# A two-layer transformer block with routed experts: choices of former tiles summed on TensorE, and the last tables loaded and added in quarters

## The chip, the cores and the metric

One core of a Trainium2 chip. The metric is the device time of one execution in microseconds (us). The engines are TensorE (PE, with its weight loads as PEld), VectorE (DVE), ScalarE (ACT), GpSimd (POOL) and SyncE (SP, which issues most DMAs).

## What is computed

1024 tokens (4 sequences of 256) of 256 features go through two layers. Each layer norms its input and adds an attention and a feed-forward part to it:

```
x = L0_attn_h                                   # (4, 256, 256), f32
xn = layernorm(x)
x = x + attention0(xn) + experts0(xn)           # 32 experts, 6 a token, 2 shared ones
xn = layernorm(x)
x = x + attention1(xn) + experts1(xn)           # 8 experts, 2 a token
return x

# experts0:  p = softmax(flat @ router_w + router_b); top 6, gates divided by their sum
#            out = mean of shared experts + sum of gate * (relu(flat @ w1 + b1) @ w2 + b2)
# experts1:  top 2 of x @ gate_kernel, softmax over the two;
#            h = silu(x @ wi_0) * (x @ wi_1) * weight;  out = h @ wo
# attention1: per token, 16 heads of q meet 8 heads of k through sine and cosine
#             features of rotated, normed vectors; the result @ Wo.T + bo
```

## The kernel before

Tokens stand in NT = 8 tiles of 128, two tiles a sequence. The kernel does not run every expert on every token. It sorts the chosen (token, expert) pairs into tiles of 128 slots of one expert each: NT0 = 79 tiles in layer 0, NT1 = 23 in layer 1. GpSimd gathers the tokens of a tile from a table in HBM (`gather_tile` L930, `gather_tile1` L1170), TensorE and ScalarE compute the expert, and GpSimd scatters the result with an addition into one of two tables of sums (`add_tile` L938, `add_tile1` L1177), tile n into table n % 2. A scatter waits for the former one on the same table.

**The routing** (`route_dve`, `rank_pe`, `route_dve_slots`, both layers; E is 32 or 8). VectorE finds each token's top experts (L264, L267), lays them out as zeros and ones (L271), and reduces them to CUM, for each tile E columns that are 1 where the token chose the expert (L274). MASKB is CUM in bf16 (L277). CUM is then summed over the tiles, each tile added to the sum of those before it, seven links (L281), and CUMB is that sum in bf16, shifted by a tile so that its first block is zero (L279, L283). `st` counts an instruction on a semaphore, and `st.link` also waits for it, so each link waits for the one before. The last conversion sets `chosen`. TensorE (`rank_pe`) then forms, in one bank, for each tile the number of earlier tokens of the tile that chose the expert (BEFOREB, a triangular matrix of ones, times the tile's block of MASKB, L377) plus those of all former tiles (ONESB, all ones, times the tile's block of CUMB, L379), and after them the total of each expert (L381), 17 matmuls in all. The last sets `rank_ok`. VectorE (`route_dve_slots`) normalises the gates (L295 to L297), waits for `rank_ok`, turns the totals into first slots of each expert (L301 to L310), and adds both up to the slot of each pair (L311 to L321). In layer 1, the rotation of queries and keys (`rope_qk`, L1074, six instructions for the first half of the tokens, each pair waiting for a square by ScalarE, L1069) stands between `route_dve` and `route_dve_slots`, and TensorE's `queries_keys` (L1063) of the second half waits for it through `qk_rp`. The slots then give the map from slot to token (L1134 to L1164), whose last instruction sets `map_ok` and lets GpSimd gather.

In layer 0, TensorE's program is: shared expert first product (L1876), its second product for two tiles `shared_down(0)` (L1884, L1885), `rank_pe`, `shared_down(1)`, the query compression (L1899), and then the map loop. In layer 1 it is: `queries_keys(0, 2)`, `rank_pe`, `queries_keys(1, 0)`.

**The end** (the last part of `layer1_dve` and the SP program). When an attention output of layer 1 has been multiplied for a sequence b (`project1`, L1349, sets `ao_ps`), VectorE adds it to the residual X (`take_project1`, L1356, 128 x 512). SP waits until all scatters of a table are in (`added[r]`) and loads the table of sums into SUMS1 in one DMA of 1 MB (L1629); it does so for both tables. VectorE does three projection adds, then adds the first table (L1490, 128 x 2048), then the second in four pieces of two tiles (L1494), each setting `f_ok`, and then the fourth projection add. SP stores each sequence when `f_ok` says so, the last when `ao_rd` says that the fourth projection is added, too (L1635).

Of the kernel before, what the change touches and what calls it, by code (L numbers as in the profile page):

```python
# [8 lines left out]
BF16 = mybir.dt.bfloat16  # L9
# [116 lines left out]
def build(nc, a, out):  # L126
# [5 lines left out]
    with ctx:  # L132
# [39 lines left out]
        MASKB = sb("chosen_bf16", NT * E0, BF16)  # L172
# [83 lines left out]
        def route_dve(dve, st, E, K, layer):  # L256
# [16 lines left out]
            st.wait()  # L273
            st.link(nc.vector.tensor_reduce(v3(CUM[:, 0:NT * E], NT),  # L274
                                            ONEH[:, 0:NT * K * E].rearrange("p (t k e) -> p t e k", t=NT, k=K),
                                            AX, ALU.add))
            st(nc.vector.tensor_copy(MASKB[:, 0:NT * E], CUM[:, 0:NT * E]))  # L277

            st.link(nc.vector.memset(CUMB[:, 0:E], 0.0))  # L279
            for t in range(1, NT):  # L280
                st.link(nc.vector.tensor_tensor(CUM[:, t * E:(t + 1) * E], CUM[:, (t - 1) * E:t * E],  # L281
                                                CUM[:, t * E:(t + 1) * E], ALU.add))
            nc.vector.tensor_copy(CUMB[:, E:(NT + 1) * E], CUM[:, 0:NT * E]).then_inc(chosen, 1)  # L283
# [89 lines left out]
        def rank_pe(pe, E, bank, layer):  # L373

            pe.wait_ge(chosen, layer + 1)
            for t in range(NT):
                nc.tensor.matmul(bank[:, t * E:(t + 1) * E], BEFOREB[:, :], MASKB[:, t * E:(t + 1) * E],  # L377
                                 start=True, stop=False)
                nc.tensor.matmul(bank[:, t * E:(t + 1) * E], ONESB[:, :], CUMB[:, t * E:(t + 1) * E],  # L379
                                 start=False, stop=True)  # L380
            nc.tensor.matmul(bank[:, NT * E:(NT + 1) * E], ONESB[:, :], CUMB[:, NT * E:(NT + 1) * E],  # L381
                             start=True, stop=True).then_inc(rank_ok, 1)
# [666 lines left out]
        sum1_ld, f_ok, f_st = [sem(f"sums1_loaded{i}") for i in range(2)], sem("f_combined"), sem("f_stored")  # L1049
# [303 lines left out]
        def take_project1(dve, b):  # L1353
            dve.wait_ge(ao_ps, b + 1)
            x = X[:, b * TPB * HID:(b + 1) * TPB * HID]
            return nc.vector.tensor_tensor(x, ps[PROJB[b % 2]][:, :], x, ALU.add).then_inc(ao_rd, 1)  # L1356
# [72 lines left out]
        def layer1_dve(dve, st):  # L1429
# [53 lines left out]
            for b in range(B - 1):  # L1483
                take_project1(dve, b)
            dve.wait_ge(ao_rd, B - 1)
            for i in range(2):
                r = (NT0 + NT1 + i) % 2
                dve.wait_ge(sum1_ld[r], 16)
                if i == 0:
                    st.link(nc.vector.tensor_tensor(X[:, :], X[:, :], SUMS1[r], ALU.add))  # L1490
                else:
                    for b in range(B):
                        x, y = (z[:, b * TPB * HID:(b + 1) * TPB * HID] for z in (X[:, :], SUMS1[r]))
                        ins = nc.vector.tensor_tensor(x, x, y, ALU.add)  # L1494
                        ins.then_inc(f_ok, 1)
            dve.wait_ge(f_ok, B)
            take_project1(dve, B - 1)


        with nc.Block() as block:  # L1500
            @block.sync
            def _(sp):
# [123 lines left out]
                for i in range(2):  # L1626
                    r = (NT0 + NT1 + i) % 2
                    sp.wait_ge(added[r], in_ring(NT0 + NT1, 2, r))
                    sp.dma_start(v3(SUMS1[r], NT), sums1[r][0:T, :].rearrange("(t p) d -> p t d", p=P)).then_inc(sum1_ld[r], 16)  # L1629
                rows = out.rearrange("b (j p) d -> b p j d", p=P)  # L1630
                for b in range(B):
                    sp.wait_ge(f_ok, b + 1)
                    if b == B - 1:
                        sp.wait_ge(ao_rd, B)
                    sp.dma_start(rows[b], x3[:, b * TPB:(b + 1) * TPB, :]).then_inc(f_st, 16)  # L1635
# [381 lines left out]
```

## Time and profile before

| | |
|---|---|
| median of three runs | 561.8 us (559.34 to 562.46) |
| the profiled execution | 560.66 us, its span 558.9 us |
| TensorE busy | 517.5 us, 93% |
| VectorE busy | 358.5 us, 64% |
| ScalarE busy | 314.5 us, 56% |
| GpSimd busy | 297.3 us, 53% |
| DMA | 90.41 MB, mean 162 GB/s |
| granted TensorE clock, mean | 0.985 |

The profile is of one execution. Busy time says how full an engine is, not what an instruction of it costs the kernel. For that one reads the chain that ended last (followed back from the last instruction, at each step to what released it) and, around a line, the timeline with the idle time that its engine had before it and who ended it. Matmuls overlap: each lasts some 0.18 us longer than the distance to the next. An f32 matmul shows as two instructions.

### The profile page before, as it was taken

To read this page: it belongs to the slowest core of one execution; us is meant where nothing else is said; L and a number is where in the kernel's file an instruction comes from. 1 tells how busy PE (TensorE), PEld (TensorE's weight loads), DVE (VectorE), ACT (ScalarE), POOL (GpSimd) and SP (SyncE) were. 2 spreads that over 40 slices of the span, in tenths; PEclk is the share of its full clock that TensorE was granted. 3 is DMA by queue.
4 is the path that set the end of the run, shared out by engine and by line. 5 is a ranking of instruction groups with operands and counts; after the bars stand their busy time and mean duration, and the time that the engine had idled before them with its cause. 6 is when DMAs were issued, how large, how long until landed. Compare 5 with 4: busy or idle time off the path is not lost.

```text
span 558.9 us, 9877 instructions
## 1 busy us (share of the span) xinstructions
PE 517.5 (93%) x2975; PEld 397.2 (71%) x2975; DVE 358.5 (64%) x1042; ACT 314.5 (56%) x739; POOL 297.3 (53%) x225
## 2 busy tenths in 40 slices
PE   7998999998989999999999999999987989899971
PEld 6566678887878888888888889888765444465561
DVE  6678827436857638457466474431685989998643
ACT  1215136776778576585776685766423358475520
POOL 1000445887767667667466577643220055888860
PEclk9699999999999999999999999999999999999997
DMA  8980636998999968578577598672677022655676
GB/s 231 376 266 1 175 91 120 227 228 217 238 267 256 245 143 185 130 157 203 112 177 165 119 204 182 156 165 30 143 225 226 1 66 58 95 94 96 90 89 225
DMA packets 87331, 90.41 MB, mean 162 GB/s; under 512 B 26736, under 2 KB 75312, under 8 KB 86896
## 3 DMA queue, kind: packets, MB, share of 16 engines
q1 hardware_dynamic: 66656, 61.50, 38.0%
q0 software_dynamic: 19584, 27.24, 28.1%
q10 hardware_dynamic: 1040, 1.05, 0.6%
q8 instruction: 25, 0.41, 0.3%
q14 instruction: 26, 0.21, 0.1%
HBM read 65.32 MB, written 22.60 MB: 157 GB/s over the span
## 4 chain that ended last, share of the span: by engine, by line
PE 54%; DMA 12%; DVE 11%; issue 11%; POOL 7%; ACT 5%; POOLq 0%; SPq 0%; ACTq 0%; DVEq 0%
PE bank L968 9%; PE bank L564 8%; DMA expert_sums<-expert_weights,token_of_slot 6%; PE bank L977 4%; PE bank L976 4%; PE bank L556 4%; PE bank L521 4%; POOL tiles L1170 3%; PE bank L1876 3%; PE bank L958 2%; POOL expert_sums L1177 2%; PE bank L539 2%; PE bank L489 2%; PE bank L509 2%; DMA expert_weights<-normed_x,token_of_slot 2%
## 5 line engine op out<-in xcount | busy, mean ns | idle before, releaser
L938 POOL DMA_INDIRECT expert_sums<-expert_weights,token_of_slot x79 | 130.2, 1649 | 59.5 <-ACT expert_weights L1000 31.5
L930 POOL DMA_INDIRECT expert_weights<-normed_x,token_of_slot x79 | 87.4, 1106 | 113.4 <-DVE token_of_slot L370 51.5
L968 PE MATMUL bank<-expert_weights 128*88 128x128 f32 x632 | 82.6, 273 | 0.4 <-ACT expert_weights L993 0.4
L968 PEld LDWEIGHTS bank<-expert_weights 128*88 128x88 f32 x632 | 72.8, 156 | 1.6 <-issue 1.6
L564 PE MATMUL bank<-out_weights,expert_weights 128*128 128x256 f32 x256 | 59.9, 380 | 2.2 <-DVE residual L827 1.5
L1177 POOL DMA_INDIRECT expert_sums<-expert_weights,token_of_slot x23 | 46.5, 2020 | 13.7 <-issue 5.9
L564 PEld LDWEIGHTS bank<-out_weights,expert_weights 128*128 128x128 f32 x256 | 46.5, 190 | 9.1 <-ACT expert_weights L675 3.8
L784 DVE SCALAR_TENSOR_TENSOR expert_weights<-bank,blocks_valid 128x64 f32<-128x64 f32 x32 | 7.1, 223 | 62.8 <-ACT expert_weights L652 62.8
L976 PE MATMUL bank<-expert_weights 88*128 88x256 f32 x158 | 47.1, 379 | 0.0
L977 PE MATMUL bank<-expert_weights 89*128 89x256 f32 x158 | 47.1, 379 | 0.0
L1000 ACT ACTIVATE expert_weights<-bank,chosen_bf 128x256 f32<-128x256 f32 x79 | 37.7, 478 | 16.3 <-PE bank L977 15.9
L1209 PE MATMUL bank<-expert_weights,tiles 128*128 x92 | 44.2, 603 | 1.3 <-DVE tiles L1259 1.3
L1170 POOL DMA_INDIRECT tiles<-normed_x,token_of_slot x23 | 23.8, 1034 | 38.8 <-DVE token_of_slot L1164 29.4
L985 ACT ACTIVATE expert_weights<-bank 128x256 f32<-128x256 f32 x79 | 30.4, 385 | 17.5 <-PE bank L958 17.5
L992 ACT ACTIVATE expert_weights<-bank,expert_weights 88x128 f32<-88x128 f32 x79 | 28.9, 366 | 18.8 <-PE bank L968 17.0
L521 PEld LDWEIGHTS bank<-keys,expert_weights 128*128 128x128 f32 x256 | 33.0, 191 | 4.6 <-issue 3.2
L521 PE MATMUL bank<-keys,expert_weights 128*128 128x112 f32 x256 | 34.0, 276 | 0.8 <-DVE expert_weights L784 0.8
L556 PE MATMUL bank<-expert_weights 112*128 112x512 f32 x64 | 33.2, 605 | 1.4 <-ACT normed L638 1.0
L946 DVE SCALAR_TENSOR_TENSOR expert_weights<-expert_weights,chosen_before_bf 128x6 f32<-128x6 f32 x79 | 15.7, 221 | 27.8 <-DMA expert_weights<-normed_x,token_of_slot 27.7
L977 PEld LDWEIGHTS bank<-expert_weights 89*128 89x128 f32 x158 | 29.9, 189 | 4.3
L637 ACT ACTIVATE tiles<-bank 128x512 f32<-128x512 f32 x32 | 19.2, 600 | 24.5 <-PE bank L489 24.4
L958 PE MATMUL bank<-ident,expert_weights 128*128 128x128 f32 x158 | 30.7, 275 | 0.0
(285 smaller groups left out, 1088.5 us busy)
## 6 DMA issues: line engine op xcount, KB each, us to landing
expert_weights<-experts_out SPq DMA_DIRECT2D x79, 192.8 KB
expert_weights<-experts_in SPq DMA_DIRECT2D x79, 176.0 KB
expert_weights<-L_ffn_wi SPq DMA_DIRECT2D x32, 128.0 KB, 2.6
expert_weights<-w_comp SPq DMA_DIRECT2D x1, 2048.0 KB, 9.4
expert_weights<-fold_g SPq DMA_DIRECT2D x1, 2048.0 KB, 13.8
expert_sums<-zeros SPq DMA_DIRECT2D x2, 1024.0 KB, 13.7
expert_weights<-L_ffn_wo SPq DMA_DIRECT2D x16, 128.0 KB, 2.6
normed<-expert_sums SPq DMA_DIRECT2D x2, 1024.0 KB, 7.1
```

The source lines that it names most:

```text
L521: ins = nc.tensor.matmul(ps[2][:, hg * NKEY:(hg + 1) * NKEY], QT[:, s * H * NSR + hg * P:s * H * NSR + (hg + 1) * P], kwin[:, b, i, :], st ...
L556: nc.tensor.matmul(ps[out_bank(t, s)][:, :], VW[b % 2][0:NKEY, i * D:(i + 1) * D], PTB[s % 2][0:NKEY, :], start=True, stop=True).then_inc( ...
L564: ins = nc.tensor.matmul(ps[7][:, 0:HID], AO[:, h * P:(h + 1) * P], wc3[:, h, :], start=(h == 0), stop=(h == H - 1))
L930: nc.gpsimd.indirect_dma_start(xt0[g % 4], None, xn0, bass.IndirectOffsetOnAxis(ap=MAP[:, g:g + 1], axis=0)).then_inc(gathered[g % 4], 16)
L938: nc.gpsimd.indirect_dma_start(sums0[g % 2], bass.IndirectOffsetOnAxis(ap=MAP[:, g:g + 1], axis=0), yt0[g % 4], None, compute_op=ALU.add). ...
L958: ins = nc.tensor.transpose(ps[1][:, k * P:(k + 1) * P], xt0[g % 4][:, k * P:(k + 1) * P], IDN[:, :])
L968: ins = nc.tensor.matmul(ps[5][0:DHB, c * P:(c + 1) * P], w[:, k * DH + c * DHB:k * DH + (c + 1) * DHB], xT0[g % NXT][:, k * P:(k + 1) * P ...
L976: nc.tensor.matmul(ps[3][:, 0:HID], hT[0:DHB, 0:P], w[0:DHB, 0:HID], start=True, stop=False)
L977: nc.tensor.matmul(ps[3][:, 0:HID], hT[0:DHB + 1, P:2 * P], w[0:DHB + 1, HID:2 * HID], start=False, stop=True).then_inc(y_ps, 1)
L1170: nc.gpsimd.indirect_dma_start(xt1[g % 4], None, xn1, bass.IndirectOffsetOnAxis(ap=MAP[:, g:g + 1], axis=0)).then_inc(gathered[n % 4], 16)
L1177: nc.gpsimd.indirect_dma_start(sums1[n % 2], bass.IndirectOffsetOnAxis(ap=MAP[:, g:g + 1], axis=0), yt1[g % 4], None, compute_op=ALU.add). ...
L1209: ins = nc.tensor.matmul(ps[HB[g % 2]][:, :], xT1[g % 3][:, k * P:(k + 1) * P], w[:, 0, k * 2 * MI:(k + 1) * 2 * MI], start=(k == 0), stop ...
```

## The change

In the routing, CUMB and the seven links go. MASKB gets one more block of E columns, set to zero. One matmul of BEFOREB with all of MASKB, the zero block too, opens the whole bank region; then for each tile t one matmul of ONESB with block t of MASKB, repeated over all later blocks (a step of zero), adds the choices of tile t to every later tile and to the totals. They are nine matmuls, 9E, 8E, 7E, ... and E columns wide. `chosen` is set by the conversion to MASKB.

At the end, each table is loaded in four DMAs of 256 KB, one for each sequence, with a semaphore each. VectorE does all four projection adds first and then adds each quarter as it lands, table by table; a quarter of the second waits for the same quarter of the first. SP's store of a sequence waits for `f_ok` alone.

```diff
--- before.py
+++ after.py
@@ -169,7 +169,7 @@
         TOPF = sb("top8_float", NT * 8)
         GATE = sb("gates", NT * K0)
         GSUM = sb("gate_sums", 2 * NT)
-        MASKB = sb("chosen_bf16", NT * E0, BF16)
+        MASKB = sb("chosen_bf16", (NT + 1) * E0, BF16)
         CUMB = sb("chosen_before_bf16", (NT + 1) * E0, BF16)
         START = sb("starts", 4 * E0)
         TEX = sb("tile_expert", NT0, I32)
@@ -271,16 +271,11 @@
                 st(nc.vector.tensor_tensor(oh[:, t], bc(IOTA[:, 0:E].unsqueeze(1), [P, K, E]),
                                            bc(tf[:, t, 0:K].unsqueeze(2), [P, K, E]), ALU.is_equal))
             st.wait()
+            st(nc.vector.memset(MASKB[:, NT * E:(NT + 1) * E], 0.0))
             st.link(nc.vector.tensor_reduce(v3(CUM[:, 0:NT * E], NT),
                                             ONEH[:, 0:NT * K * E].rearrange("p (t k e) -> p t e k", t=NT, k=K),
                                             AX, ALU.add))
-            st(nc.vector.tensor_copy(MASKB[:, 0:NT * E], CUM[:, 0:NT * E]))
-            st.link(nc.vector.memset(CUMB[:, 0:E], 0.0))
-            for t in range(1, NT):
-                st.link(nc.vector.tensor_tensor(CUM[:, t * E:(t + 1) * E], CUM[:, (t - 1) * E:t * E],
-                                                CUM[:, t * E:(t + 1) * E], ALU.add))
-            nc.vector.tensor_copy(CUMB[:, E:(NT + 1) * E], CUM[:, 0:NT * E]).then_inc(chosen, 1)
+            nc.vector.tensor_copy(MASKB[:, 0:NT * E], CUM[:, 0:NT * E]).then_inc(chosen, 1)
 
             nc.vector.tensor_tensor(g3, tp[:, :, 0:K], bc(tp[:, :, 0:1], [P, NT, K]), ALU.subtract).then_inc(gates_sub, 1)
 
@@ -373,13 +368,12 @@
         def rank_pe(pe, E, bank, layer):
 
             pe.wait_ge(chosen, layer + 1)
+            nc.tensor.matmul(bank[:, 0:(NT + 1) * E], BEFOREB[:, :], MASKB[:, 0:(NT + 1) * E], start=True, stop=False)
             for t in range(NT):
-                nc.tensor.matmul(bank[:, t * E:(t + 1) * E], BEFOREB[:, :], MASKB[:, t * E:(t + 1) * E],
-                                 start=True, stop=False)
-                nc.tensor.matmul(bank[:, t * E:(t + 1) * E], ONESB[:, :], CUMB[:, t * E:(t + 1) * E],
-                                 start=False, stop=True)
-            nc.tensor.matmul(bank[:, NT * E:(NT + 1) * E], ONESB[:, :], CUMB[:, NT * E:(NT + 1) * E],
-                             start=True, stop=True).then_inc(rank_ok, 1)
+                later = bank[:, (t + 1) * E:(NT + 1) * E].rearrange("p (n e) -> p n e", e=E)
+                ins = nc.tensor.matmul(later, ONESB[:, :], bc(MASKB[:, t * E:(t + 1) * E].unsqueeze(1), [P, NT - t, E]),
+                                       start=False, stop=(t == NT - 1))
+            ins.then_inc(rank_ok, 1)
 
         def layernorm_stats(dve, st, tiles):
 
@@ -1046,7 +1040,8 @@
         MAPC = 128
 
         x1_st, hst, hld = sem("normed1_stored"), sem("b_heads_stored"), [sem(f"b_heads_loaded{b}") for b in range(B)]
-        sum1_ld, f_ok, f_st = [sem(f"sums1_loaded{i}") for i in range(2)], sem("f_combined"), sem("f_stored")
+        part_ok = sem("first_sums_added")
+        sum1_ld, f_ok, f_st = [[sem(f"sums1_loaded{i}_{b}") for b in range(B)] for i in range(2)], sem("f_combined"), sem("f_stored")
         (qk_ps, qk_sq, qk_rp, vr_ps, vr_ok, ang_ps, at_sb, an_ps, ssum, root, u_ok, apart, sines, squared, o_ok, oT_ps, oT_sb, ao_ps, ao_rd) = (
             sem("b_" + n) for n in (
                 "qk_psum", "qk_squares", "qk_turned", "v_psum", "v_ready", "angles_psum", "angles_sbuf", "anglesT_psum", "square_sums", "roots", "turns",
@@ -1480,21 +1475,17 @@
                         turns(dve, st, part + 1)
             assert 3 * NT >= NT1
 
-            for b in range(B - 1):
+            for b in range(B):
                 take_project1(dve, b)
-            dve.wait_ge(ao_rd, B - 1)
+            dve.wait_ge(ao_rd, B)
             for i in range(2):
                 r = (NT0 + NT1 + i) % 2
-                dve.wait_ge(sum1_ld[r], 16)
-                if i == 0:
-                    st.link(nc.vector.tensor_tensor(X[:, :], X[:, :], SUMS1[r], ALU.add))
-                else:
-                    for b in range(B):
-                        x, y = (z[:, b * TPB * HID:(b + 1) * TPB * HID] for z in (X[:, :], SUMS1[r]))
-                        ins = nc.vector.tensor_tensor(x, x, y, ALU.add)
-                        ins.then_inc(f_ok, 1)
-            dve.wait_ge(f_ok, B)
-            take_project1(dve, B - 1)
+                for b in range(B):
+                    dve.wait_ge(sum1_ld[r][b], 16)
+                    if i:
+                        dve.wait_ge(part_ok, b + 1)
+                    x, y = (z[:, b * TPB * HID:(b + 1) * TPB * HID] for z in (X[:, :], SUMS1[r]))
+                    nc.vector.tensor_tensor(x, x, y, ALU.add).then_inc(f_ok if i else part_ok, 1)
 
 
         with nc.Block() as block:
@@ -1626,12 +1617,12 @@
                 for i in range(2):
                     r = (NT0 + NT1 + i) % 2
                     sp.wait_ge(added[r], in_ring(NT0 + NT1, 2, r))
-                    sp.dma_start(v3(SUMS1[r], NT), sums1[r][0:T, :].rearrange("(t p) d -> p t d", p=P)).then_inc(sum1_ld[r], 16)
+                    for b in range(B):
+                        sp.dma_start(v3(SUMS1[r], NT)[:, b * TPB:(b + 1) * TPB, :],
+                                     sums1[r][b * S:(b + 1) * S, :].rearrange("(j p) d -> p j d", p=P)).then_inc(sum1_ld[r][b], 16)
                 rows = out.rearrange("b (j p) d -> b p j d", p=P)
                 for b in range(B):
                     sp.wait_ge(f_ok, b + 1)
-                    if b == B - 1:
-                        sp.wait_ge(ao_rd, B)
                     sp.dma_start(rows[b], x3[:, b * TPB:(b + 1) * TPB, :]).then_inc(f_st, 16)
                 sp.wait_ge(f_st, 16 * B)
```

## Rows read from the trace of the kernel before

**Rows 1.** The page, part 4: the chain that ended last, by engine.

```profile
PE 54%; DMA 12%; DVE 11%; issue 11%; POOL 7%; ACT 5%; POOLq 0%; SPq 0%; ACTq 0%; DVEq 0%
```

**Rows 2.** Timeline, 20 to 60 us: start, duration, engine, line, [idle before, releaser].

```profile
29.16 0.29 DVE L283 CAST chosen_before_bf<-expert_weights 128x256 bf16<-128x256 f32 x1
...
32.25 0.18 PE L377 MATMUL bank<-chosen_bf,before_bf 128*128 128x32 bf16 x1
...
32.65 0.18 PE L381 MATMUL bank<-chosen_before_bf,ones_bf 128*128 128x32 bf16 x1
...
32.87 0.19 DVE L301 TENSOR_SCALAR starts<-bank 128x32 f32<-128x32 f32 x1 [2.31 <-PE bank L381]
```

**Rows 3.** Timeline, 426 to 475 us.

```profile
430.87 0.69 ACT L1069 ACTIVATE keys<-bank,shared_w 128x512 f32<-128x512 f32 x1 [1.03 <-PE bank L1063]
431.10 0.20 DVE L277 CAST chosen_bf<-out_weights 128x64 bf16<-128x64 f32 x1
...
432.77 0.20 DVE L283 CAST chosen_before_bf<-out_weights 128x64 bf16<-128x64 f32 x1
432.87 0.17 DVE L285 TENSOR_TENSOR gates<-top 128x16 f32<-128x16 f32 x1
432.96 0.74 DVE L1074 SCALAR_TENSOR_TENSOR expert_weights<-bank,shared_w 128x512 f32<-128x512 f32 x1
...
433.02 0.18 PE L377 MATMUL bank<-chosen_bf,before_bf 128*128 128x8 bf16 x1 [2.18 <-DVE chosen_before_bf L283]
...
434.42 3.70 PE L1063 MATMUL bank<-normed,expert_weights 128*128 128x512 f32 x8 [0.81 <-DVE q_up_weights L1074]
```

**Rows 4.** The chain in order of time, 431 to 438.2 us: start, duration, what.

```profile
431.36 0.18 DVE out_weights L281
```

**Rows 5.** Timeline of GpSimd, 440 to 545 us.

```profile
450.09 1.12 POOL L1170 DMA_INDIRECT tiles<-normed_x,token_of_slot  x1 [29.42 <-DVE token_of_slot L1164]
```

**Rows 6.** The same timeline, one tile of the long middle.

```profile
487.21 0.99 POOL L1170 DMA_INDIRECT tiles<-normed_x,token_of_slot  x1 [0.30 <-issue]
488.51 2.52 POOL L1177 DMA_INDIRECT expert_sums<-expert_weights,token_of_slot  x1 [0.30 <-issue]
```

**Rows 7.** The chain in order of time, 540 to 559 us.

```profile
541.82 3.61 DMA expert_sums<-expert_weights,token_of_slot
...
545.44 7.49 DMA normed<-expert_sums
```

**Rows 8.** Timeline, 522 to 562 us.

```profile
545.26 1.99 PE L1349 MATMUL bank<-expert_weights 128*128 128x256 f32 x8 [0.69 <-ACT expert_weights L1341]
550.20 2.29 DVE L1490 TENSOR_TENSOR residual<-residual,normed 128x2048 f32<-128x2048 f32 x1 [6.13 <-DMA normed<-expert_sums]
553.03 2.50 DVE L1494 TENSOR_TENSOR residual<-residual,normed 128x512 f32<-128x512 f32 x4 [0.54 <-DMA normed<-expert_sums]
...
555.56 0.69 DVE L1356 TENSOR_TENSOR residual<-bank,residual 128x512 f32<-128x512 f32 x1
```

**Rows 9.** Stretches: length, busy of five engines, granted clock, DMA share, GB/s.

```profile
412.00:424.00 12.00, 11.08 (x66) 9.46 (x65) 7.34 (x21) 2.37 (x7) 3.56 (x5) 1.00 0.86 262
547.00:551.00 4.00, 0.25 (x2) 0.00 (x0) 0.80 (x1) 0.00 (x0) 0.00 (x0) 1.00 1.02 341
```

**Rows 10.** DMA issues within 400 to 432 us: count, KB each, us to landing.

```profile
expert_weights<-L_ffn_wi SPq DMA_DIRECT2D x24, 128.0 KB, 2.5
...
normed_x<-normed SPq DMA_DIRECT2D x1, 128.0 KB, 5.4
```

**Rows 11.** Timeline, 47 to 56 us: six f16 matmuls of 79 columns.

```profile
47.09 0.40 PE L360 MATMUL bank<-expert_weights 128*128 128x79 f16 x6 [0.44 <-DVE expert_weights L347]
```

**Rows 12.** Timeline of SP: its issues, 385 to 559 us.

```profile
412.10 0.91 SPq L1529 DMA_DIRECT2D expert_weights<-L_ffn_wi  x2
...
543.38 2.44 SPq L1629 DMA_DIRECT2D normed<-expert_sums  x2
```

**Rows 13.** The line of the four stores of the result (L1635): us to landing.

```profile
DMA to landing us min/median/max: 2.1/2.3/2.5
```

## Prediction, made before the changed kernel had run

> **What bounds the kernel now.** I read the page first: TensorE has 54% of the chain that ended last [rows 1], but each of the three places that the change touches has its own bound, so I read each in the timeline and in the chain.
>
> First place, the ranks of layer 0 [rows 2]. VectorE ends its sums over former tiles (L281, L283) at 29.45 us, but TensorE is still in the shared expert's second product and issues the first rank matmul only at 32.25. VectorE has stood idle 2.31 us, put down to the last rank matmul (L381), when it goes on at 32.87. TensorE, not VectorE, comes last here.
>
> Second place, the ranks of layer 1 [rows 3]. The roles are exchanged. TensorE has been idle 2.18 us when L283 releases it at 433.02, and VectorE runs without a gap: L277, L279, seven L281, L283, L285, then six L1074 (the rotation of queries and keys). The seven links stand in the chain, 0.18 and 0.02 each [rows 4]. VectorE stays the bound until L1164 has the map; GpSimd, idle 29.42 us, then starts its first gather at 450.09 [rows 5]. From there GpSimd paces the experts, in the long middle some 4.1 us a tile: gather 0.99, scatter 2.52, two gaps of 0.3 [rows 6].
>
> Third place, the end. The last scatter lands at 545.44, the second table takes 7.49 us to land, to 552.93 [rows 7], and only then come four adds of 0.68, one projection add of 0.69, and the last store, at 556.3. The projection's matmuls L1349 were over at 547.25, so the last L1356 stands at 555.56 only because the code puts it last [rows 8]. The DMA engines are full from 547 to 551, at 341 GB/s [rows 9].
>
> **Part 1: VectorE's work for the ranks.** Removed are the memset of CUMB, seven linked adds and one conversion; added is a memset of the last E columns of MASKB, ahead of the reduction. In layer 1, L285 now follows L283 by 0.10 us, and I let it follow L277 by the same: 431.20 in place of 432.87, 1.67 us. Between L277's end (431.30) and the first link (431.36) the old memset had 0.06, and I charge the new one as much. That leaves 1.6 us. What is late next? The first two squares are ready before the third, which ends at 431.56; the third is wanted by the fifth rotation, at about 434.0 [rows 3]. TensorE wants `chosen`, now at about 431.35, and was idle since 430.84. Its next matmul, L1063 at 434.42, is released by the second rotation (`qk_rp`), so it moves by the same 1.6, and with it all that TensorE does up to the map. The stores of normed_x that the gather also awaits are issued within the window of [rows 10], ending at 432, and land in 5.4 us at most, well before 448; the expert loads stand ahead of them in SP's queue. So everything behind VectorE moves as a block: map, gathers, GpSimd's rhythm, heads, last scatter. I take 1.6 us off, bounds 0 (the block stopped by something the trace doesn't show) and 1.7.
>
> In layer 0 the same removal frees VectorE of as many instructions, and ACT issues its store of normed_x a little sooner, since its exponential follows L285. The rank matmuls do not start sooner, being queued behind the shared expert's: worth 0. If that cover were gone, it would be worth the same 1.6 to 1.9.
>
> **Part 2: the rank matmuls.** 17 matmuls of E columns become 9, of 9E, 8E, 7E, down to E columns. In layer 0 that is 17 x 32 = 544 columns before and 288 + 1152 = 1440 after. The narrow ones start 0.025 us apart, 0.40 from first to last [rows 2]. A wide bf16 matmul isn't in the trace. Nearest are six f16 ones of 79 columns, 0.40 us from the first start to the last end; one alone lasts about as long as a narrow one, 0.18 to 0.2, so the other five add 0.04 each or 0.51 ns a column [rows 11]. At that price the nine take 0.73 us, 0.3 longer. Bounds: width for nothing (9 x 0.025, so 0.2 shorter), and the price of f32, four matmuls of 256 columns in 1.99 [rows 8], so 1.9 ns a column and 2.8 us, 2.4 longer. I take +0.3, since f16 has the width of bf16. It stands on the path: L301 awaits it, and the slots and the map follow on VectorE. The shared expert's next product, queued behind it on TensorE, is read only inside the map loop. In layer 1 the sum is 360 columns, 0.7 us even at the f32 price; it starts at about 431.4 and nobody waits for it before L1063 (about 432.8) and L301: 0.
>
> **Part 3: the end.** One load of a table becomes four, of 256 KB each, with a semaphore each; the sum over the first table becomes four adds of 0.68 in place of one of 2.29, +0.4 us on a VectorE that is idle for 6.13 us until 550.20 [rows 8]. All four projection adds come first, the last at about 547.3. Its new place has only table adds behind it, and no table is there before 550. Behind the last landing stand one add of 0.68, the issue 0.1 later, and the store. Before, 552.93 to 556.3 for the issue is 3.4 us; after, 0.8. Saving 2.6 us.
>
> SP issues eight DMAs for two. Loads of 128 KB are issued 0.475 us apart (three in some 1.4), so the first table's four, from 543.38, take until about 545.2, just under the wait for the second at 545.44, whose last is issued at 546.9 [rows 12], long before the engines get to it. Behind them on SP are only the stores.
>
> Do the quarters land as fast? Whole tables move at 341 GB/s with full engines. The 128 KB loads move 262 GB/s at a busy share of 0.86, so 305 at full share [rows 9]. Two tables of 1.05 MB take 6.1 us at the one rate and 6.9 at the other: 0 to 0.8 later. A quarter of 256 KB lies between, and I take +0.3. No row excludes a gain, but bytes and 1 KB rows are the same, so I allow 0.1 of it. The first three stores stand behind the loads in SP's queue, need 0.8 us each, and are through by about 554.6; the last, issued about 554.0 on the old clock, then takes its 2.3 to 2.5 us [rows 13]: 0, at most +0.4. Part 3 is -2.6 + 0.3 = -2.3 (bounds -2.7 and -1.4).
>
> The Trainium skill ("DMA: Bandwidth & Descriptors", section "Bandwidth") speaks against this part: DMAs should be batched to 1 MiB or more. Its section "Anatomy of one DMA" gives each DMA about 2.0 us fixed plus the bytes at 436 GB/s; by that an estimate for a quarter is 2.6 us, and four that did not overlap would take 10.4 in place of 4.4 for the table. The stores of 256 KB in this trace do overlap: they are issued as their adds end, 0.68 apart, and each lands in 2.1 to 2.5.
>
> **The sum.** -1.6 + 0 + 0.3 + 0 - 2.3 = -3.6 us. The profiled execution took 560.66 us (span 558.9 and 1.8 around it), which gives 557.1. The timed runs are 559.34, 561.8 and 562.46; with the profiled one their mean is 561.1, between profile and median. I take 561.1 - 3.6 = 557.5.
>
> **The rivals.** *B, the early stores mix with the loads* on the engines and push the last quarter back by three stores, 0.79 MB at 341 GB/s, 2.3 us. For: the engines are full. Against: the stores are issued behind all loads, on the same queue. Part 3 is then 0, the whole -1.3: 559.8. *C, layer 1's shift stops*: gather or scatter rhythm is held by something that does not move. For: GpSimd's scatters take longer at some times than at others, so they depend on what runs beside them. Against: the 29.42 us of idle end with L1164. Then 0.3 - 2.3 = -2.0: 559.1. *D, wide matmuls over a repeated operand run at the f32 price*: +2.4 in place of +0.3, the whole -1.5: 559.6. *E, slower*: each quarter pays its own landing, one behind another. Eight times 2.3 us [rows 13] from 543.38 reach 561.8, 8.9 later than 552.93; with the 1.3 and 2.6 won elsewhere that is +5.0: 566.1. It costs more than is won from (552.93 - 543.38 + 3.9) / 8 = 1.7 us a quarter on, against 0.8 at the full rate. The 128 KB loads, issued 0.475 apart and landing in 2.5 [rows 10, 12], speak against it. The skill's fixed cost, read as a cost in sequence, would be this rival.
>
> **How the numbers follow.** Forecast 0.70, B 0.12, C 0.08, D 0.04, E 0.06. About 0.5% (2.8 us) is what a measurement of this kernel can tell from no change. Of the forecast's 0.70, 0.05 falls within that by the scatter of medians (three runs spread over 3.1 us). So faster 0.65, same 0.05 + 0.24 = 0.29, slower 0.06. The range: the favourable ends are -1.7 + 0 - 2.7 = -4.4, which from the lowest run, 559.34, is 555.0; upward it takes in B, C and D from the highest run, 562.46 - 1.3 = 561.2. E is left out.
>
> **What the profile after would show.** (1) In layer 1, L281 and L283's conversion gone, and L277 to the first L1074 down from 1.86 us to about 0.2. (2) From L277 of layer 1 to the first gather 17.4 in place of 19.0, and from that gather to the last scatter 91.7 as before. (3) In layer 0, first rank matmul to L301 up from 0.62 to about 0.9. (4) From the last scatter's landing to the last table landing 7.5 to 7.8, then one add and one store, 3.4 us to the end in place of 6.0. Wrong would be: quarters landing over 1 us apart, a gather that does not come sooner, or a scatter rhythm that stretches.

## The result, and the profile after

Over 17 executions of each, the changed kernel has a median of 557.02 us (555.48 to 559.53) against 561.62 us (558.36 to 564.96). The ratio is 0.9923 with a 95% interval of 0.9907 to 0.9939, so 4.3 us less, between 3.4 and 5.2. The profiled execution has a span of 555.3 us against 558.9, which is 3.6 less. So the pair of profiles shows the forecast 3.6, which lies within the interval, and the times a little more. The experiments ask whether the 3.6 is made up as forecast, and whether there is a rest.

The chain that ended last, by engine, has shifted from DMA to TensorE against [rows 1]; it is the fourth part of the page of after:

```profile
PE 58%; DVE 11%; issue 10%; DMA 8%; POOL 7%; ACT 5%; SPq 0%; POOLq 0%; ACTq 0%; DVEq 0%
```

That tells where the last release came from and no more; the three places have to be read one by one.

Layer 0. The timeline of after, 27 to 34 us (start, duration, engine, line, shapes, [idle before, releaser]):

```profile
32.28 0.29 PE L371 MATMUL bank<-chosen_bf,before_bf 128*128 128x288 bf16 x1
32.40 0.66 PE L374 MATMUL bank<-chosen_bf,ones_bf 128*128 128x256 bf16 x8
...
33.10 0.19 DVE L296 TENSOR_SCALAR starts<-bank 128x32 f32<-128x32 f32 x1 [3.60 <-PE bank L374]
```

L371 and L374 stand in the place of L377 to L381. From the first rank matmul to VectorE's next instruction it is 0.82 us, where [rows 2] have 0.62. VectorE is freed earlier and idles 3.60 us in place of 2.31.

Layer 1. The timeline of after, 429 to 436 us, the lines that answer to [rows 3]:

```profile
431.73 0.20 DVE L278 CAST chosen_bf<-out_weights 128x64 bf16<-128x64 f32 x1
431.84 0.17 DVE L280 TENSOR_TENSOR gates<-top 128x16 f32<-128x16 f32 x1
431.92 0.74 DVE L1069 SCALAR_TENSOR_TENSOR expert_weights<-bank,shared_w 128x512 f32<-128x512 f32 x1
431.98 0.21 PE L371 MATMUL bank<-chosen_bf,before_bf 128*128 128x72 bf16 x1 [0.53 <-DVE chosen_bf L278]
...
433.38 2.84 PE L1058 MATMUL bank<-normed,expert_weights 128*128 128x512 f32 x6 [1.01 <-DVE q_up_weights L1069]
```

The links are gone: from the bf16 copy to the first rotation it is 0.19 us, before it was 1.86. TensorE idles 0.53 us ahead of the ranks, not 2.18, and 1.01 us behind them, where it was 0.81.

The timeline of GpSimd in after, its first gather and last scatter ([rows 5] have the first gather of before):

```profile
449.06 1.12 POOL L1165 DMA_INDIRECT tiles<-normed_x,token_of_slot  x1 [27.75 <-DVE token_of_slot L1159]
...
541.09 1.55 POOL L1172 DMA_INDIRECT expert_sums<-expert_weights,token_of_slot  x1 [1.44 <-DMA expert_sums<-expert_weights,token_of_slot]
```

The end. The chain of after in order of time, 535 to 556 us, for [rows 7]:

```profile
541.09 3.92 DMA expert_sums<-expert_weights,token_of_slot
...
546.46 5.17 DMA normed<-expert_sums
551.63 0.03 issue
551.65 0.69 DVE residual L1488
```

and the timeline of after, 534 to 556 us, for [rows 8]:

```profile
542.48 4.45 SPq L1621 DMA_DIRECT2D normed<-expert_sums  x8
...
544.50 1.99 PE L1344 MATMUL bank<-expert_weights 128*128 128x256 f32 x8 [0.69 <-ACT expert_weights L1336]
546.53 0.69 DVE L1351 TENSOR_TENSOR residual<-bank,residual 128x512 f32<-128x512 f32 x1 [3.28 <-PE bank L1344]
547.26 5.08 DVE L1488 TENSOR_TENSOR residual<-residual,normed 128x512 f32<-128x512 f32 x8
550.39 2.36 SPq L1626 DMA_DIRECT2D out<-residual  x4
```

Behind the last landing stands one add. But VectorE runs its eight table adds without a gap from 547.26 on: it is no longer idle there.

Laid end to end, the two profiles differ so:

| stretch | before | after | difference |
|---|---|---|---|
| start to the bf16 copy of layer 1 | 431.10 | 431.73 | +0.63 |
| bf16 copy to first gather | 18.99 | 17.33 | -1.66 |
| first gather to last scatter's issue | 91.73 | 92.03 | +0.30 |
| last scatter's issue to last table landing | 11.11 | 10.54 | -0.57 |
| last landing to the end of the span | 5.97 | 3.67 | -2.30 |
| span | 558.9 | 555.3 | -3.6 |

Of the +0.63, 0.24 is there when layer 0's map is ready (53.59 and 53.83). The rest is within what one execution differs from another: over the profiles of all kernels below, the bf16 copy of layer 1 lies between 430.0 and 432.8, whatever their ranks. The -0.57 is of that kind too, as the section on the tables' loads shows.

### The profile page after: what moved, and what is told of

Its sections match the earlier page's. It is cut to its first block, busy times and chain, and to the rows that moved or that the text cites. A ratio compares the mean times of both kernels' runs of the same rounds, so it can differ in the third digit from the quotient of the medians.

```text
span 555.3 us, 9839 instructions
## 1 busy us (share of the span) xinstructions
PE 517.5 (93%) x2959; PEld 397.1 (72%) x2959; DVE 355.6 (64%) x1029; ACT 313.9 (57%) x739; POOL 297.9 (54%) x225
## 4 chain that ended last, share of the span: by engine, by line
PE 58%; DVE 11%; issue 10%; DMA 8%; POOL 7%; ACT 5%; SPq 0%; POOLq 0%; ACTq 0%; DVEq 0%
PE bank L962 10%; PE bank L558 9%; PE bank L971 5%; PE bank L970 5%; PE bank L550 4%; PE bank L515 4%; DMA expert_sums<-expert_weights,token_of_slot 3%; POOL tiles L1165 3%; PE bank L1867 3%; PE bank L952 2%; PE bank L533 2%; PE bank L483 2%; PE bank L503 2%; DMA expert_weights<-normed_x,token_of_slot 2%; POOL expert_sums L1172 2%
```

## The experiments

All ratios are against the kernel before; each with its 95% interval.

### The two parts alone

`e1_ranks_only` is before with the new `route_dve` and `rank_pe` in both layers. `e2_end_only` is after with the old ones.

> Only the ranks of the change, in both layers; the end is that of before. Theory: layer 1 wins the 1.67 us between the bf16 copy and the first rotation, layer 0 loses 0.2, and both arrive at the end, so 1.3 to 1.5 us below before (ratio about 0.9975), with first gather of layer 1 to last scatter unchanged at 91.7 to 92.1. Rival (layer 1's shift stops on the way, as the last scatter landed only 0.4 us sooner in the trace of after): 0 to +0.3 us against before.

> Only the end of the change; the ranks are those of before. Theory: the end as traced after (from the last scatter's landing to the end of the span 10.3 us in place of 13.5), so 3.0 to 3.2 us below before (ratio about 0.9945). The prediction's sum had 2.3. Rival (the ranks do nothing, all of the 4.6 us is the end): 4.3 to 4.6 us below before.

Measured: ranks only 0.9951 (0.9927 to 0.9975), 2.8 us less, between 1.4 and 4.1. End only 0.9981 (0.9958 to 1.0004), 1.1 us less, between 2.4 less and 0.2 more. The spans of their profiles are 557.0 and 556.7. In ranks only it is 17.33 us from copy to gather, and from the last landing to the end 5.9. In end only it is 18.99 and 3.5. So each part does in the trace what it does in after, and the rivals (shift lost, all of the gain at the end) fall. The times don't share the gain as this pair of traces does. The end's theory of 3.0 to 3.2 us lies outside its interval: it took the end of before from one profile, whose end is longer than in the other profiles with the same end (see the tables' loads). The ranks have 2.8 where the traces give 1.4 (1.66 less 0.24), just at the edge of their interval; the points alone don't prove that anything is missing, but they say where to look.

### Projections in front alone

```diff
-            for b in range(B - 1):
+            for b in range(B):
                 take_project1(dve, b)
-            dve.wait_ge(ao_rd, B - 1)
+            dve.wait_ge(ao_rd, B)
...
-            dve.wait_ge(f_ok, B)
-            take_project1(dve, B - 1)
```

SP's wait for `ao_rd` ahead of the last store goes, too.

> Before, with nothing but the fourth projection add moved ahead of the table adds; whole tables in one DMA each, one add of 2.29 for the first, four for the second, last store waits for its quarter alone. Theory: takes 0.69 from behind the last landing (3.37 us to the last issue become 2.7), so 0.7 us below before; the rest of the gain at the end is the quarters' (three adds of 0.68, about 2.0). Rival (the order of the adds is the gain and not the quarters): 2 us or more below before.

Measured 0.9992 (0.9970 to 1.0013), 0.4 us less, with an interval that holds both 0 and the 0.7. The rival's 2 us are excluded. In the trace the landing is followed by 5.7 us to the end, 0.3 less than before: the last store's issue ends 0.78 sooner, and some 0.5 is given back between the end of that issue and the end of the span (2.7 in place of 2.2). But this profile was the find. Its stretches, 435 to 439 us (length, busy of the five engines, granted clock, DMA share, GB/s):

```profile
435.00:436.00 1.00, 0.90 (x1) 0.39 (x2) 1.00 (x3) 0.00 (x0) 0.00 (x0) 0.63 0.00 0
436.00:437.00 1.00, 1.00 (x3) 0.47 (x2) 1.00 (x3) 0.00 (x0) 0.00 (x0) 0.50 0.00 0
437.00:438.00 1.00, 1.00 (x3) 0.48 (x2) 0.96 (x4) 0.00 (x0) 0.00 (x0) 0.50 0.00 0
438.00:439.00 1.00, 1.00 (x2) 0.29 (x2) 0.80 (x6) 0.19 (x1) 0.00 (x0) 0.67 0.00 0
```

and from its timeline TensorE's two first instructions there:

```profile
433.71 0.18 PE L377 MATMUL bank<-chosen_bf,before_bf 128*128 128x8 bf16 x1 [2.18 <-DVE chosen_before_bf L283]
...
435.10 5.40 PE L1063 MATMUL bank<-normed,expert_weights 128*128 128x512 f32 x8 [0.81 <-DVE q_up_weights L1074]
```

The clock is granted at 0.5, so 1.2 GHz, for 3.4 us, right after TensorE has idled 2.18 and 0.81 us around the old ranks of layer 1. The same eight L1063 take 5.40 us, and 3.70 in [rows 3], and from copy to gather it is 20.30 us in place of 18.99.

### The clock

`e10_idle_filled` is before, with TensorE kept at work in that idle time:

```diff
+            for n in range(4):
+                nc.tensor.matmul(ps[1][:, 0:HID], IDN[:, :], xnT3[:, 0, 0:HID], start=True, stop=True)
             rank_pe(pe, E1, ps[2], 1)
+            nc.tensor.matmul(ps[1][:, 0:HID], IDN[:, :], xnT3[:, 0, 0:HID], start=True, stop=True)
```

> Before, with five f32 matmuls of 256 columns (0.43 us each, into a bank that nobody reads then) added in TensorE's idle time around the ranks of layer 1: four ahead of them, one behind; the computation is unchanged. In one of the three profiles with the old ranks (the one with only the projections in front) the clock was granted at 0.66 on average from 435 to 440 us, right after that idle time, and the first gather came 1.3 us later than in the two others. Clock theory: the old ranks' idle time, 2.18 and 0.81 us, costs in some executions a spell at 1.2 GHz, the new ranks' doesn't; filled, it is gone: 0.3 to 1 us below before, granted clock 1.00 in the whole stretch from 430 to 450. Rival (the one profile was an accident that has nothing to do with the idle time): within 0.2 us of before.

`e11_links_doubled` lengthens the idle time instead:

```diff
+            if layer == 1:
+                for t in range(1, NT):
+                    st.link(nc.vector.tensor_tensor(START[:, 3 * E0:3 * E0 + E], START[:, 3 * E0:3 * E0 + E],
+                                                    START[:, 3 * E0:3 * E0 + E], ALU.add))
             nc.vector.tensor_copy(CUMB[:, E:(NT + 1) * E], CUM[:, 0:NT * E]).then_inc(chosen, 1)
```

> Before, with seven more linked adds of E columns (on a scratch region that nothing reads) on VectorE ahead of layer 1's conversion, so that TensorE's idle time there is 3.6 us in place of 2.18. The computation is unchanged. Both theories have the 7 x 0.20 = 1.4 us of VectorE on the path. Clock theory (an idle TensorE there costs a spell at 1.2 GHz, so far in 2 of 4 profiles with the old ranks unfilled, and it cost 1.1 to 1.3 us up to the first gather): the spell now comes in nearly every execution, so 1.4 + about 0.6 = 2.0 us above before, and this profile has it. Rival (the spells are accidents of other origin): 1.4 us above before, and the profile as likely without one as with.

Measured: filled 0.9989 (0.9967 to 1.0010), 0.6 us less, and links doubled 1.0034 (1.0005 to 1.0064), 1.9 us more. Both agree with the clock theory's numbers (0.3 to 1 less, 2.0 more), but neither interval excludes the rival's (0, and 1.4 more). The clock itself decides more than the times do. Filled, the timeline has

```profile
434.22 0.18 PE L377 MATMUL bank<-chosen_bf,before_bf 128*128 128x8 bf16 x1 [0.46 <-DVE chosen_before_bf L283]
...
435.62 3.70 PE L1063 MATMUL bank<-normed,expert_weights 128*128 128x512 f32 x8 [0.28 <-DVE q_up_weights L1074]
```

and doubled

```profile
434.69 0.19 PE L381 MATMUL bank<-chosen_bf,before_bf 128*128 128x8 bf16 x1 [3.60 <-DVE chosen_before_bf L287]
436.08 5.83 PE L1067 MATMUL bank<-normed,expert_weights 128*128 128x512 f32 x8 [0.79 <-DVE q_up_weights L1078]
```

with the clock, in the stretches of links doubled, down while TensorE still stands idle:

```profile
433.00:434.00 1.00, 0.00 (x0) 0.00 (x0) 0.83 (x5) 0.00 (x0) 0.00 (x0) 0.79 0.00 0
434.00:435.00 1.00, 0.32 (x12) 0.32 (x12) 0.90 (x5) 0.22 (x1) 0.00 (x0) 0.50 0.00 0
...
439.00:440.00 1.00, 1.00 (x3) 0.48 (x2) 0.81 (x6) 0.10 (x1) 0.00 (x0) 0.50 0.00 0
440.00:441.00 1.00, 1.00 (x3) 0.29 (x2) 0.90 (x9) 0.59 (x1) 0.00 (x0) 0.80 0.00 0
```

All fourteen profiles of this study together, over the stretch from 430 to 445 us:

| TensorE's idle time ahead of layer 1's ranks | profiles | with a spell at 1.2 GHz | copy to first gather |
|---|---|---|---|
| 0.53 us (new ranks) | after and six experiments | 0 of 7 | 17.33 in each |
| 0.46 us (old ranks, filled) | e10 | 0 of 1 | 18.99 |
| 2.18 us (old ranks) | before, e2, e3, e5, e8 | 3 of 5 (e3, e5, e8) | 18.99 without, 20.07 to 20.30 with |
| 3.60 us (old ranks, links doubled) | e11 | 1 of 1 | 22.14 |

Doubled, the 18.99 grow by 1.40 of links and by 1.75 of slower TensorE. With the new ranks the idle time behind them is 1.01 us, and no spell came either.

Five profiles are few, but the timed executions have their mean granted clock on record, too. Here are all that the ratios of the experiments rest on, and the 17 of after; the profiles without a spell have a mean of 0.985 to 0.987, those with a short one 0.980 to 0.983:

| kernels | executions | mean granted clock | of them at 0.982 or less |
|---|---|---|---|
| old ranks in layer 1: before, e2, e3, e5, e8 | 140 | 0.9811 | 88 |
| new ranks in layer 1: after, e1, e4, e6, e7, e9, e12 | 79 | 0.9852 | 9 |
| old ranks, idle time filled: e10 | 12 | 0.9848 | 0 |
| old ranks, links doubled: e11 | 12 | 0.9781 | 9 |

This leaves no room for the rival, a spell by accident: five matmuls in the idle time give the clock back, and a longer idle time costs more of it. (Nine executions with the new ranks are as low, so something else moves the mean a little, too.) It is layer 1's ranks, since e6, with the old ones in layer 0, has 0.9843, and it isn't the end, since e2, with the new end, has 0.9822 and e1, with the old one, 0.9858.

What the clock costs in time is less certain. At 3 in 5, a spell of 1.1 to 1.3 us is 0.7 us a mean execution. The recorded clocks hint at more: 0.0041 of 560 us is 2.3 us of full clock lost, where a spell of 3.4 us at half the clock loses 1.7, and at the profiles' price that is an estimate of 1.6 us. Filling the idle time gave 0.6 us less, between 1.9 less and 0.6 more. So I put what the new ranks save by the clock, beside their 1.66, at an estimated 0.6 to 1.6 us. With 1.66 - 0.24 that makes 2.0 to 3.0 us for the ranks, within the interval of ranks only.

### Layer 0's order

`e4_ranks_first` is after, and `e5_before_ranks_first` is before, each with

```diff
+                rank_pe(pe, E0, ps[3], 0)
                 pe.wait_ge(sh_sb, 4)
                 shared_down(0)
-                rank_pe(pe, E0, ps[3], 0)
```

> After, with layer 0's rank matmuls issued before the shared expert's second product. In after, TensorE idles 0.77 us there (to 28.71) with chosen set at 27.53, and VectorE idles 3.60 us to 33.10. Theory: the nine matmuls fit into that idle time, VectorE goes on at about 29.5 and the map is ready about 3 us sooner; the long stretch to layer 1 is paced by TensorE, so 2 to 3.5 us below after (6.5 to 8 below before, ratio about 0.987). Rival (TensorE's own work up to the map, 21 us of it, is the bound, so the sooner slots only move idle time): 0 to 0.7 us below after.

> Before, with layer 0's rank matmuls issued ahead of the shared expert's second product. With the new ranks that order gave nothing: VectorE went on at 29.91 in place of 33.10, but the map was ready at 53.59 as ever, since TensorE's own work and the map loop's waits reach to there. With the old sums TensorE must also wait for them (chosen at 29.45, TensorE free at 27.9), which puts 1.3 us of idle time into TensorE. Theory (TensorE is the bound up to the map): map ready 0.5 to 1.3 us later than in before, time 0.3 to 1.3 above before. Rival (VectorE is the bound): VectorE goes on at about 30.3, map ready up to 2 us sooner. It also gives one more look at the clock with the old ranks in layer 1.

Measured: e4 0.9927 (0.9901 to 0.9954), as after; e5 0.9996 (0.9972 to 1.0020), as before. In e4 VectorE goes on 3.2 us sooner than in after, and the map is ready at 53.59, as in before. Its waits from 30 to 54 us show why (who waited for whom, us in total, times, longest):

```profile
DVE expert_weights L340 <- ACT expert_weights L349: 2.9, 1, 2.9
PEld bank L355 <- DVE expert_weights L342: 2.8, 5, 0.8
```

VectorE, with its second tile's buffers laid, waits 2.9 us for ScalarE (L349), and the chain leads from there through `shared_relu(4)` to TensorE's shared products and L1890, which follow each other without idle time from 29.19 to 41.54. So my theory of 2 to 3.5 us fell, and its rival holds: up to the map TensorE's own work is as long as VectorE's way. In e5 it is 27.09 us from bf16 copy to map against 26.36 in before, 0.7 later, as the theory there had it; the time doesn't resolve it.

`e6_layer1_only` keeps the old ranks in layer 0 (`if layer == 1:` around the new code).

> After, with the old sums and rank matmuls in layer 0 and the new ones in layer 1 only. Theory: layer 0's nine wide matmuls cost 0.2 us on VectorE's path (first rank matmul to VectorE's next instruction 0.62 against 0.82), so this kernel is 0.2 us below after, first rank matmul to map 21.3 us in place of 21.5; layer 1 as in after, first gather 17.3 us behind the bf16 copy. Rival (the freed VectorE of layer 0 is worth something after all, by the earlier store of normed_x): 0.3 us or more above after.

Measured 0.9913 (0.9877 to 0.9948), to be set beside after's 0.9923: the point is 0.6 us lower (the median, 557.47 against 557.02, is higher), in an interval 4 us wide, which decides neither for the theory's 0.2 us below nor against the rival's 0.3 above. In its trace VectorE goes on 0.62 us after the first rank matmul, the map is ready 21.34 us after it (21.55 in after), and it is 17.33 us from copy to gather, so both halves do what they do elsewhere. No time here shows that any of the versions beats after.

### The tables' loads and the stores

`e8_quarter_loads_only` is before with four DMAs a table and VectorE's order untouched, `e7_eighths` is after with one DMA of 128 KB a tile, and VectorE's waits count two DMAs a quarter:

```diff
-                        sp.dma_start(v3(SUMS1[r], NT)[:, b * TPB:(b + 1) * TPB, :],
-                                     sums1[r][b * S:(b + 1) * S, :].rearrange("(j p) d -> p j d", p=P)).then_inc(sum1_ld[r][b], 16)
+                        for t in range(b * TPB, (b + 1) * TPB):
+                            sp.dma_start(v3(SUMS1[r], NT)[:, t:t + 1, :],
+                                         sums1[r][t * P:(t + 1) * P, :].rearrange("(j p) d -> p j d", p=P)).then_inc(sum1_ld[r][b], 16)
```

> Before, with each table loaded in four DMAs of 256 KB, and VectorE as in before (it awaits all four of a table). Whole tables landed 8.5 to 9.6 us after the first load's issue in the traces, quarters 9.1 to 9.6. Theory (size of DMA costs nothing): last landing 9.0 to 9.6 us after the first issue, time within 0.3 us of before. Rival (the prediction's +0.3, up to +0.8, for smaller DMAs): 0.3 to 0.8 us above before. The two lie close, so the trace decides more than the time.

> After, with one DMA of 128 KB a tile, 16 in all, and the adds in quarters as in after. Doubles what smaller DMAs may cost: SP's issues then take 16 x 0.47 = 7.5 us from the first (542.5 to 550), so the last one is issued 3.5 us later than in after. Theory: SP's issuing becomes the bound, last landing about 10 us after the first issue in place of 9.15, so +0.5 to +1.5 us against after. Rival (the engines pace it anyway): within 0.3 us of after.

Measured: e8 1.0005 (0.9979 to 1.0030), no difference. From the first load's issue to the last landing, six profiles with whole tables have 9.55, 8.45, 9.31, 8.92, 8.97 and 8.72 (before, e1, e3, e5, e11, e10), mean 8.99, and six with quarters 9.15, 9.57, 9.06, 9.24, 9.10 and 9.09 (after, e2, e4, e8, e9, e6), mean 9.20. (In e12, below, nobody waits for the last quarter, so its landing can't be read.) The difference of 0.2 is smaller than the spread among whole tables, so all that is shown is that a price for smaller DMAs, if there is one, is small.

At 9.55, before's own profile has the longest of the six with whole tables, and its last table took the longest from the last scatter's landing, 7.49 us against 5.54 to 6.67 in the five others. So it makes the end of before look longer than it mostly is. From the first load's issue to the end of the span, five profiles with the old end (before, e1, e5, e10, e11) take 15.5, 14.4, 14.8, 14.6 and 14.9, mean 14.85, and four with the new end (after, e2, e4, e6) 12.8, 13.1, 12.6 and 12.6, mean 12.77. The change at the end is worth 2.1 us by these, not the 2.9 (0.57 + 2.30) of the one pair, and 2.1 is within the interval of end only.

e7 has 0.9944 (0.9917 to 0.9972), 1.2 us above after by the ratios, though the intervals overlap, and the end of its chain reads

```profile
549.78 3.20 DMA normed<-expert_sums
552.98 0.02 issue
553.00 0.69 DVE residual L1488
```

The first of its 16 loads was issued at 542.75, so the last landed 10.23 us later, where after has 9.15; it was issued only at 549.31, behind 15 issues of 0.43 and 0.04. At 128 KB SP's issuing is the bound, at 256 KB it isn't.

`e9_stores_held` is after with one line ahead of the stores, `sp.wait_ge(sum1_ld[(NT0 + NT1 + 1) % 2][B - 1], 16)`.

> After, with SP's stores held until the last quarter of the second table has landed. In after the first store is issued at 550.39, 1.24 us ahead of that landing. Theory: early stores do not slow the loads and the last store is issued by its own add, but then all four come within about 1.5 us and the last waits for three: 0.3 to 1 us above after. Rival B of the prediction (stores on their way slow the loads down): last landing sooner than 9.15 us after the first issue and the time at or below after.

Measured 0.9958 (0.9934 to 0.9982), 2.0 us above after by the ratios and 0.8 by the medians, so the theory's 0.3 to 1 is not decided by the time. The last landing comes 9.10 us after the first issue, as with free stores (9.15), so the early stores don't push the last quarter back by the 2.3 us of the prediction's rival B: it is out. The last landing to the end takes 4.87 us in place of 3.67, of which 2.9 follow the end of the last issue (2.5 in after, 2.2 in before).

`e12_first_table_before` moves the fourth projection add behind the first table's adds.

> After, with the fourth projection add moved behind the adds of the first table (still ahead of the second's). In after VectorE idles until 546.53 for that projection while the first quarter has landed at about 545.7, and then runs eight adds without a gap, 547.26 to 552.34. Theory that VectorE paces the end: it starts 0.9 us sooner, the last add ends up to 0.5 us sooner, time 0.2 to 0.5 below after. Rival (the last landing paces it, 551.63 in after): last add unchanged, time within 0.1 us of after.

Measured 0.9924 (0.9896 to 0.9951), as after. Its VectorE timeline:

```profile
546.58 0.69 DVE L1490 TENSOR_TENSOR residual<-residual,normed 128x512 f32<-128x512 f32 x1 [2.06 <-DMA normed<-expert_sums]
547.92 0.69 DVE L1490 TENSOR_TENSOR residual<-residual,normed 128x512 f32<-128x512 f32 x1 [0.65 <-DMA normed<-expert_sums]
548.80 1.39 DVE L1490 TENSOR_TENSOR residual<-residual,normed 128x512 f32<-128x512 f32 x2 [0.19 <-DMA normed<-expert_sums]
550.22 0.69 DVE L1351 TENSOR_TENSOR residual<-bank,residual 128x512 f32<-128x512 f32 x1
550.95 2.55 DVE L1490 TENSOR_TENSOR residual<-residual,normed 128x512 f32<-128x512 f32 x4
```

The early adds now wait for their quarters instead, 0.65 and 0.19, and the last add ends 10.0 us after the first load's issue, in after 9.9. Nothing is won; landings and adds are equally late there.

## Why the prediction was right

**Part 1** was right in size and place. The 1.6 us are 1.66, and the shift went through to the gather as a block, 17.33 us from copy to gather in each of seven profiles. Rival C, the shift that stops, is out. What the step missed stood in its own rows: [rows 3] show TensorE idle 2.18 and 0.81 us, and I read this only as proof that the ranks were not late, not as a risk for the clock. The profile of before happened to have no spell. The missed term is the clock. The sum had nothing for it; the traces and the recorded clocks of the timed executions show its sign and mechanism, and its size is an estimate, 0.6 to 1.6 us. That the timed gain (4.3) exceeds that of the profiles (3.6) by 0.7 does not measure it, since the interval of the time would allow for none. That VectorE's work in layer 0 was worth nothing is borne out by e4: even with VectorE going on 3.2 us sooner, the map is ready only 0.2 us sooner (53.59 against 53.83).

**Part 2** had +0.3 and measured +0.2. The eight repeated matmuls have 1152 columns and span 0.66 us with 0.18 of it the last one's tail, so 0.48 for the 1120 columns ahead of it, 0.43 ns a column, where I had taken 0.51 from the f16 rows. The f32 price of D would have been 1.9 ns a column: D is out.

**Part 3** had -2.6 for the work behind the last landing and +0.3 for the loads. Behind the landing it is -2.30: SP's last issue is 2.65 sooner relative to it, but from the end of that issue to the end of the span it takes 2.5 us in place of 2.2. What fits is that the three stores in front are closer to it and still on their way: issued closer still, in e9, it takes 2.9. I had given this 0 with a bound of +0.4. The loads cost +0.2 by twelve profiles, less than their spread. Together that is -2.1, for the forecast -2.3. What I had wrong is the base of this part: I took the 7.49 us from the last scatter's landing to the last table's as what it always takes and forecast 7.5 to 7.8 after. After has 6.62, and the other kernels with whole tables 5.54 to 6.67, so this sign of the prediction failed, though no term of its sum hangs on it. One thing was read wrongly without harm: I had VectorE done with the first table's adds as that table lands. In after the projection add keeps them back until 547.26, all eight run behind each other, and the last begins the moment its quarter is there. One more add, or a slower one, should then cost time, which no run here tries.

**The rivals.** E, quarters one behind another, would have shown landings 2.3 us apart. The eight quarters were all down in 9.2 us. The Trainium skill ("DMA: Bandwidth & Descriptors", section "Bandwidth") asks for DMAs of 1 MiB and more; with eight of 256 KB queued behind each other the difference is 0.2 us in 9, within the scatter of the profiles, so here the measurement decides against the rule. The prediction's estimate of 2.6 us for a quarter goes by the Trainium skill's section "Anatomy of one DMA", which describes DMAs issued by GpSimd, and these loads are issued by SP; no run here has a quarter alone. The Trainium skill's section "Issuing engines are not separate DMA queues", on the same page, says that issuing is usually short against the DMA itself; at 128 KB, e7 shows it as the bound.

**The sum.** Base 561.1 and -3.6 gave 557.5; the median is 557.02, against 561.62 for before. Base and difference were off by 0.5 and 0.7 to 1, in opposite directions, so that the time came out nearer than its parts: that is luck. Luck is also in the exact 3.6 of the pair of profiles. Stretch by stretch, what the runs support is -1.66 + 0.24 - 2.08 = -3.5 without the clock, and 4.1 to 5.1 us less with it, against 4.3 measured; in the pair, an end of before that was 0.8 too long is made up by +0.4 ahead of layer 1's ranks and +0.3 between first gather and last scatter, which come and go with the execution.

## What to carry to other kernels

A chain of small linked vector steps can become matmuls that accumulate into a bank, but it pays only where the chain comes last: 1.7 us in layer 1, and -0.2 in layer 0, where TensorE was late anyway. When an edit ends an idle time of TensorE of a few us, look at the granted clock of several executions, not of one: here TensorE was slower afterwards in some executions only, and the mean clock of the timed executions told it more clearly than their times. Compare a stretch over several profiles, too, before its difference is put down to a change. At a kernel's end, cut the last load so that one short step and one store follow its last piece, and stop cutting where the issuing queue becomes the bound.

## What was not expected of the hardware

- After an idle time of TensorE of 2.18 us, 17 small matmuls and another 0.81 us, the granted clock fell to 0.5 (1.2 GHz) for 3.4 us in 3 of 5 profiled executions, and in the others not at all. With 3.60 us it fell in the one profile taken, while TensorE still stood idle, for 6.8 us; with about 0.5 us ahead of the ranks it fell in none of eight. The eight matmul halves that follow take 5.2 to 5.4 us in place of 3.7, and 5.8 after the longest idle time. The mean granted clock of the timed executions was 0.9811 with the idle time and 0.9848 with it filled.
- bf16 matmuls whose moving operand repeats a block with a step of zero ran at 0.43 ns a column, at 256 to 32 columns each.
